# Batch 1's norm and transposes moved ahead, high parts multiplied first, and a gate buffer for each batch in the scan stage of a decoder layer

## What is computed

```python
x = x + _L0_attn_ref(_layernorm(x), W_in, conv_w, conv_b, W_g, b_g, forget_base, W_out)
# inside, H = 384:
gx = einsum('ntd,hd->nth', x, W_in);  gate, xb = gx[..., :H], gx[..., H:]
xb = depthwise_causal_conv(xb, conv_w, conv_b)            # 4 taps along t
fg = einsum('nth,gh->ntg', xb, W_g) + b_g;  forget, inp = fg[..., :H], fg[..., H:]
alpha = exp(-8 * softplus(forget_base) * sigmoid(forget))
beta = sqrt(1 - alpha ** 2 + 1e-6)
h = linear_scan(alpha, beta * sigmoid(inp) * xb)          # h[t] = alpha[t] h[t-1] + x[t]
return einsum('nth,dh->ntd', gelu(gate) * h, W_out)
# then: cross attention (AFT, local) with its MLP, and two layers of windowed attention with MLP
```

## Time and profile before

| what | us |
|---|---|
| median of three runs | 992.8 |
| lowest and highest run | 991.03, 993.05 |
| span of the profiled execution (its own whole time is not listed) | 990.8 |
| PE busy in the span | 924.9 |
| DVE, ACT, POOL busy | 675.9, 513.9, 422.6 |

### The profile page before, as it was taken

One profiled execution on the slowest core, in us unless ns is written; L12 is line 12 of the kernel. 1 busy time (PEld: TensorE's weight loads), 2 busy tenths in 40 slices (PEclk: granted clock), 3 DMA queues, 4 the chain that ended last, 5 costly groups with the idle time before them and its releaser, 6 DMA issues.

```text
span 990.8 us, 17519 instructions
## 1 busy us (share of the span) xinstructions
PE 924.9 (93%) x5688; PEld 774.2 (78%) x5688; DVE 675.9 (68%) x1706; ACT 513.9 (52%) x1221; POOL 422.6 (43%) x420
## 2 busy tenths in 40 slices
PE   5889996999999988999999899999999999889998
PEld 4668875787878866888888678887888888778887
DVE  6878797558687677677767555567766667735563
ACT  5467751313131426767666644454766666654443
POOL 5333354112221357767676400006776767631110
PEclk9889998999999999999999999999999999999999
DMA  7200123000000000000001030000000000000001
GB/s 261 70 1 16 48 65 112 1 1 0 0 0 1 1 23 1 2 23 0 22 0 33 12 105 15 4 25 2 2 24 0 22 0 12 27 15 17 31 25 46
DMA packets 15716, 26.34 MB, mean 27 GB/s; under 512 B 1642, under 2 KB 12256, under 8 KB 14896
## 3 DMA queue, kind: packets, MB, share of 16 engines
q1 hardware_dynamic: 15664, 25.69, 8.0%
HBM read 20.53 MB, written 2.10 MB: 23 GB/s over the span
## 4 chain that ended last, share of the span: by engine, by line
PE 72%; DVE 11%; ACT 6%; issue 3%; POOL 3%; SPq 3%; DMA 2%; ACTq 0%; DVEq 0%; POOLq 0%
PE bank L1593 33%; PE bank L1941 5%; PE bank L1895 5%; PE bank L1919 5%; PE bank L1801 5%; PE bank L1905 4%; ACT probs L1460 3%; PE bank L1764 2%; PE bank L1882 2%; PE bank L1747 1%; SPq L352 1%; DVE y L820 1%; PE bank L1929 1%; PE bank L2014 1%; PE bank L2011 1%
## 5 line engine op out<-in xcount | busy, mean ns | idle before, releaser
L1460 ACT ACTIVATE probs<-bank,row_min 128x256 f32<-128x256 f32 (+1 forms) x256 | 110.4, 458 | 120.1 <-DVE row_min L1048 120.1
L569 POOL TENSOR_TENSOR norms<-norms,minus_half 128x16 f32<-128x16 f32 x32 | 93.6, 2924 | 2.7
L1048 DVE CUSTOM_DVE_ANT_0 bank<-bank,mask 128x256 f32<-128x256 f32 (+1 forms) x256 | 90.7, 425 | 5.9 <-PE bank L1895 5.7
L1593 PE MATMUL bank<-wqkv_hi,x_hi 128*128 128x512 f32 x192 | 82.4, 429 | 1.8 <-DVE rot L1024 1.1
L1593 PE MATMUL bank<-wqkv_lo,x_hi 128*128 128x512 f32 x192 | 76.3, 397 | 0.0
L1593 PE MATMUL bank<-wqkv_hi,x_lo 128*128 128x512 f32 x192 | 75.7, 394 | 0.0
L1185 DVE SCALAR_TENSOR_TENSOR hidden<-bank,lcols,hidden 128x512 f32<-128x512 f32 (+1 forms) x48 | 36.0, 749 | 51.9 <-PE bank L1593 28.2
L551 POOL TENSOR_TENSOR q_tok<-rot 128x512 f32<-128x512 f32 x32 | 41.2, 1288 | 57.7 <-DVE rot L1024 57.7
L1905 PE MATMUL bank<-ident,probs 128*128 128x128 f32 x448 | 61.5, 279 | 3.9 <-ACT probs L1460 3.9
L1593 PE MATMUL bank<-t_hi,wm_hi 128*128 128x512 f32 x160 | 63.6, 397 | 0.0
L1593 PE MATMUL bank<-t_lo,wm_hi 128*128 128x512 f32 x160 | 63.5, 397 | 0.0
(11 more groups left out here) (253 smaller groups left out, 2639.5 us busy)
## 6 DMA issues: line engine op xcount, KB each, us to landing
w_stage<-in_wm_l_dram SPq DMA_DIRECT2D x8, 534.0 KB, 3.7
w_stage<-in_wqkv_dram SPq DMA_DIRECT2D x2, 1536.0 KB, 8.0
out_dram<-stream SPq DMA_DIRECT2D x8, 256.0 KB, 2.4
emb<-in_ctx_dram SPq DMA_DIRECT2D x1, 1536.0 KB, 6.8
inner<-in_w_gate_dram SPq DMA_DIRECT2D x1, 1152.0 KB, 10.3
stream<-in_x_dram SPq DMA_DIRECT2D x2, 512.0 KB, 5.7
stream<-in_x_dram SPq DMA_DIRECT2D x1, 1024.0 KB, 12.8
ew<-in_pos_bias_dram SPq DMA_DIRECT2D x1, 1024.0 KB, 11.5
```

The source lines that it names most:

```text
L569: pool.tensor_tensor(norms[:, 2, :], norms[:, 1, :], minus_half[:, :], ALU.pow).then_inc(c_rn, 1)
L1048: dve.tensor_tensor_reduce(logits, logits, mask[:, 2 * P - nk:2 * P], 1.0, FAR, ALU.add, ALU.min, row_min[:, w % 2, 2 * i + e:2 * i + e + ...
L1460: act.activation(probs[:, i, e, 0:nk], logits, ACT.Exp, bias=row_min[:, w % 2, h:h + 1], scale=-1.0, accum_out=row_sum[:, w % 2, h:h + 1]) ...
L1593: ins = pe.matmul(out, stationary, moving, start=(first and i == 0), stop=(last and i == len(terms) - 1))
```

## The change

It has five parts.

1. The gate has four buffers, one for each batch. The two new ones are slices of `w_stage`, which holds nothing in this stage (its first transfer waits for the last `output`). ACT's wait for `a_gh` is gone.
2. Batch 1's `norm_stats` and `rstd_of` stand earlier, and so does its `norm_apply`. POOL begins the split of the gate weight only when all of batch 1 is normed (`n_norm`, 2 * TT).
3. PE transposes batch 1 after the fourth input product of batch 0, no longer after the sixth. ACT rounds it into `t_hi` before the last gelu of batch 0, after waiting for all of batch 0's input products, which read `t_hi`.
4. The first input product of every batch (`first_input`) multiplies the four pairs with a high part of the tokens first, and the two with the low part last. It waits for each part by itself; before, all six waited for both low parts. Batch 0's transposes go token tile by token tile, each as soon as its tile is normed.
5. DVE takes `conv_taps(0, 2)` ahead of `conv_low(0, 0)`.

```diff
+        gate_acts = [gate_act[:, i, :, :] for i in range(2)]
+        gate_acts += [w_stage[:, i * KR * T:(i + 1) * KR * T].rearrange(...) for i in range(2)]
...
             rstd_of(0)
+            rstd_of(1)
+            pool.wait_ge(n_norm, 2 * TT)
             pool.wait_ge(wg_in, 16)
             for k in range(KR):
-                if k == 1:
-                    rstd_of(1)
                 raw_k = w_raw[:, WIN_COLS + k * 2 * RH:WIN_COLS + (k + 1) * 2 * RH]
...
                 if i == 1:
                     low_part(0, a_tp_out, a_tp_lo)
-
-            dve.wait_ge(x1_in, 16)
-            dve.wait_ge(a_tp, 2)
-            norm_stats(1, 1)
+                    dve.wait_ge(x1_in, 16)
+                    norm_stats(1, 1)
+
+            dve.wait_ge(a_tp, KD)
+            norm_apply(1, 1, False)
...
-            norm_apply(1, 1, False)
             conv_taps(0, 0)
             conv_taps(0, 1)
             low_part(1, a_tp_out, a_tp_lo)
+            conv_taps(0, 2)
             conv_low(0, 0)
-            conv_taps(0, 2)
             conv_low(0, 1)
...
-            def gelu_gate(b):
-                if b > 1:
-                    act.wait_ge(a_gh, 3 * b - 3)
-                for j in range(KR):
+            def gelu_gate(b, js=range(KR)):
+                for j in js:
                     act.wait_ge(a_in, 6 * b + KR + j + 1)
-                    act.activation(gate_act[:, b % 2, j, :], ...)
+                    act.activation(gate_acts[b][:, j, :], ...)
...
             taps(0)
-            gelu_gate(0)
+            gelu_gate(0, range(KR - 1))
+            act.wait_ge(a_in, 2 * KR)
             transposed_out(1)
+            gelu_gate(0, range(KR - 1, KR))
...
+            def first_input(b, m):
+                for k in range(KD):
+                    pe.wait_ge(a_tp_out, KD * b + k + 1)
+                    if b == 0:
+                        pe.wait_ge(win_hi, k + 1)
+                    pe.matmul(bank[2], w_in_hi[:, k, m], t_hi[:, k], start=(k == 0), stop=False)
+                for k in range(KD):
+                    if b == 0:
+                        pe.wait_ge(win_lo, k + 1)
+                    pe.matmul(bank[2], w_in_lo[:, k, m], t_hi[:, k], start=False, stop=False)
+                for k in range(KD):
+                    pe.wait_ge(a_tp_lo, KD * b + k + 1)
+                    ins = pe.matmul(bank[2], w_in_hi[:, k, m], t_lo[:, k], ..., stop=(k == KD - 1))
             def inputs(b):
-                pe.wait_ge(a_tp_lo, 2 * b + 2)
                 for j in range(2 * KR):
+                    if b == 0 and j == 4:
+                        transpose_in(1)
```

More of the change, by code:

```diff
@@ L145, in build @@
         gate_act = sb("gate_act", [P, 2, KR, T], stack=st1)
+        gate_acts = [gate_act[:, i, :, :] for i in range(2)]
+        gate_acts += [w_stage[:, i * KR * T:(i + 1) * KR * T].rearrange("p (j t) -> p j t", j=KR) for i in range(2)]
         th_in = sb("th_in", [P, KR, T], stack=st1)
@@ L426, in gate_products @@
                     pool.wait_ge(a_scan, 3 * b + j + 1)
-                    pool.tensor_tensor(scanned[:, j, :], scanned[:, j, :], gate_act[:, b % 2, j, :], ALU.mult)\
+                    pool.tensor_tensor(scanned[:, j, :], scanned[:, j, :], gate_acts[b][:, j, :], ALU.mult)\
                         .then_inc(a_gh, 1)
@@ L749, in recurrence @@
                     dve.wait_ge(a_scan, 3 * b + j + 1)
-                    dve.tensor_tensor(scanned[:, j, :], scanned[:, j, :], gate_act[:, b % 2, j, :], ALU.mult)\
+                    dve.tensor_tensor(scanned[:, j, :], scanned[:, j, :], gate_acts[b][:, j, :], ALU.mult)\
                         .then_inc(a_gh, 1)
@@ L1274, in taps @@
                         .then_inc(a_tap0, 1)
-            def gelu_gate(b):
-                if b > 1:
-                    act.wait_ge(a_gh, 3 * b - 3)
-                for j in range(KR):
+            def gelu_gate(b, js=range(KR)):
+                for j in js:
                     act.wait_ge(a_in, 6 * b + KR + j + 1)
-                    act.activation(gate_act[:, b % 2, j, :], bank[2 + (KR + j) % 4][:, :], ACT.Gelu).then_inc(a_gelu, 1)
+                    act.activation(gate_acts[b][:, j, :], bank[2 + (KR + j) % 4][:, :], ACT.Gelu).then_inc(a_gelu, 1)
             act.wait_ge(w1s_in, 16)
@@ L1597, in transpose_in @@
             def transpose_in(b):
-                pe.wait_ge(n_norm, 4 * b + 4)
-                for c in range(KD):
-                    for t in range(TT):
+                if b:
+                    pe.wait_ge(n_norm, 4 * b + 4)
+                    pe.wait_ge(a_tp_lo, KD * b)
+                    for c in range(KD):
+                        for t in range(TT):
+                            ins = pe.transpose(bank[c][:, t * P:(t + 1) * P], normed[:, t, c * P:(c + 1) * P],
+                                               ident[:, :])
+                        ins.then_inc(a_tp, 1)
+                    return
+                for t in range(TT):
+                    pe.wait_ge(n_norm, t + 1)
+                    for c in range(KD):
                         ins = pe.transpose(bank[c][:, t * P:(t + 1) * P], normed[:, t, c * P:(c + 1) * P],
                                            ident[:, :])
-                    ins.then_inc(a_tp, 1)
+                        if t == TT - 1:
+                            ins.then_inc(a_tp, 1)
+            def first_input(b, m):
[3 more added lines that the diff above has]
+                        pe.wait_ge(win_hi, k + 1)
+                    pe.matmul(bank[2][:, :], w_in_hi[:, k, m * P:(m + 1) * P], t_hi[:, k, :], start=(k == 0), stop=False)
+                for k in range(KD):
+                    if b == 0:
+                        pe.wait_ge(win_lo, k + 1)
+                    pe.matmul(bank[2][:, :], w_in_lo[:, k, m * P:(m + 1) * P], t_hi[:, k, :], start=False, stop=False)
+                for k in range(KD):
+                    pe.wait_ge(a_tp_lo, KD * b + k + 1)
+                    ins = pe.matmul(bank[2][:, :], w_in_hi[:, k, m * P:(m + 1) * P], t_lo[:, k, :], start=False,
+                                    stop=(k == KD - 1))
+                ins.then_inc(a_in, 1)
             def inputs(b):
-                pe.wait_ge(a_tp_lo, 2 * b + 2)
                 for j in range(2 * KR):
                     m = (j + KR) % (2 * KR)
+                    if b == 0 and j == 4:
+                        transpose_in(1)
                     if b == 1 and j < 2:
@@ L1618, in inputs @@
                         pe.wait_ge(a_tap0, 3 * b + j - 4 + 1)
-                    if b == 0 and j % KR == 0:
-                        pe.wait_ge(win_lo, KD * (j // KR + 1))
+                    if j == 0:
+                        first_input(b, m)
+                        continue
+                    if b == 0 and j == KR:
+                        pe.wait_ge(win_lo, 2 * KD)
                     product(bank[2 + j % 4][:, :], [
@@ L1667, in _ @@
             inputs(0)
-            transpose_in(1)
             inputs(1)
```

## The result

The changed kernel takes 983.66 us, the median of four runs (982.97 to 986.82), beside 991.91 us (989.44 to 993.05) for the kernel before, also four runs. The comparison gives a ratio of 0.9942, with a 95% interval of 0.9922 to 0.9961. That is 5.7 us faster, by the interval 3.9 to 7.7. The two medians by themselves lie further apart, 8.2 us. I had forecast 6.5 us and 986.3 us, with a range of 982.0 to 990.2. The profiled execution has a span of 981.2 us.

The account below looks back on a forecast made before the run. PE, busy for 93% of the span, was taken as the bound, with time to gain only in its idle and half-clock stretches. Gate buffers 5.4 + front 1.1 = 6.5 us, so 992.8 - 6.5 = 986.3 us; range 982.0 to 990.2.

Parts of the forecast that it names:

- The bound: Scan stage: PE works 93% of the span, so time can come only where it idles or runs at half clock.
- Part 1: Gate buffers: the 2.95 us gelu wait and 2.9 of half clock go, a 0.4 wait comes; gain 5.4 us.
- Part 2: Batch 1's norm comes 7.0 us earlier, but POOL's split then blocks DVE's taps; t_lo ends at 29.2, so nothing is gained.
- The rule of the page: Front taps: under an exclusive DVE/GpSimd port lock, t_lo of batch 1 is ready at 30.4, the forecast about 0.6 us later.
- POOL's split: Gate-weight split on POOL: delayed to about 25.5 from 22.85 us; PE needs it at 38, so nobody waits.
- Parts 3 and 4: Front, batch 1's input products: four matmuls run before the pause, the end comes at 38.1 instead of 39.2; gain 1.1 us.
- Part 5: Taps before conv_low: conv_lo ready at about 35.2, long before PE's 38.1; costed at nothing.
- The sum: Whole program: 5.4 + 1.1 = 6.5 us, from 992.8 to 986.3 us.
- DVE holds batch 1: Rival, chance 0.14: PE waits at batch 3's transposes, the gate buffers bring only 2.95; sum 4.0, 988.8 us.
- Nothing is left: Rival, chance 0.09: front loses 1.0 us, gate buffers keep 2.95 less 1.5 for DVE late at batch 3; 992.3 us.
- Slower: Rival, chance 0.05: POOL's split makes DVE 8.1 us late to batch 3's norm, PE waits 2.7 us; 995.5 us.
- The front opens: Rival, chance 0.08: taps blocked little, t_lo ready before PE asks, front brings up to 7.5; sum 12.9, 979.9 us.

Follow-up runs that it names:

- e6: The changed kernel without POOL's three subtractions for the gate weight's low part, which is set to zero and missing from the result: 978.42 us, ratio 0.9882.
- e8: The changed kernel with the gate-weight split taken off POOL: ACT rounds, DVE subtracts, and POOL makes batch 2's rstd earlier: 978.28 us, ratio 0.9880.
- e1: The kernel before with only the four gate buffers added and ACT's wait for a_gh removed: 986.14 us, ratio 0.9951.
- e3: The kernel before with twelve more matmuls, result unused, where PE waits for batch 2's gelu; the wait itself stays: 988.37 us, ratio 0.9984.
- e4: The changed kernel without POOL's wait for n_norm ahead of the gate-weight split: 984.92 us, ratio 0.9934.
- e7: The changed kernel with POOL's gate-weight split put off until DVE has made its first six taps: 980.65 us, ratio 0.9902.
- e2: The changed kernel with the two old gate buffers and ACT's wait for a_gh put back: 988.92 us, ratio 0.9977.
- e5: The changed kernel with each batch's first input product waiting for both t_lo before any of its matmuls: 986.19 us, ratio 0.9958.

## Why the prediction was right, step by step

- **The bound.** Right. Both places that I named are where the runs find the time: the front (up to 6 us more, e6 to e8) and the gelu wait (5.1 us, e1).
- **Part 1, 5.4 us forecast.** The traces show 5.1 from `gates(0)` to `output(0)`, in the changed kernel and in e1. The terms: the wait of 2.95 is gone. The half clock cost 2.6 (2.55 by e3), where I had 2.9. I took 27 x 0.234 from 9.19 and left out two things that full clock has too: the second matmul after a pause starts 0.34 us behind the first (67.48 to 67.82 in e3), 0.1 more than the 0.234 of the others, and the last of a row ends 0.39 us after its start, which adds 0.16. Together these are the 0.3. The new wait for `normed` is 0.47, where I had 0.4.
- **Part 2, nothing left of 7.0 us.** Right, with two misses that cancel, so that 29.2 is closer than its terms. `normed` ended at 16.79, not 16.0: the statistics began at 11.84, not 11.5, and POOL's `var_eps` and `rstd` took 0.41 and 1.21 us, not the 1.2 together that they took before (0.19 and 1.01). They stand beside `w_in_lo`, which I had put there myself and at no cost. The block of the taps cost less than I took. From the end of `normed` to the end of the taps it is 11.34 us (16.79 to 28.13), where I had 11.95. POOL's first rounding (0.84) met only the little `fb_tmp`, which lost 0.6 us. `t_lo` ended at 29.32 us, forecast 29.2. That 29.2 was right for the reason given is shown by e4 (the same 29.46 with the block on `normed`) and by e6 and e7 (the block taken away).
- **The rule of the page.** By the Trainium skill, "SBUF — State Buffer", a blocked instruction of DVE's, with two inputs in SBUF as the taps have, would start only after the whole of the other, and `t_lo` would have come at 30.4. The first tap ended 0.56 us after POOL, near (0.53), not 0.75, and `t_lo` came at 29.32. The trace agrees with the page on the block, and not on its last 0.2 us.
- **POOL's split.** Forecast to end at 25.5, it ended at 26.57. 0.8 us of that is its later start (16.88, not 16.1). Here a step failed: I said only that the block lengthens DVE. POOL is lengthened as well, 0.84 to 1.29 and 1.85 to 2.15 us, when it comes while a tap of DVE's is under way. Its six durations add up to 9.5 us instead of 8.1. My 25.5 had 1.3 us more than 16.1 + 8.1, for which I gave no term. This cost nothing, as said, since PE reads the split only at 38 us.
- **Parts 3 and 4, 1.1 us forecast.** `gates(0)` came at 38.31 us, forecast 38.1, and 39.18 before: 0.87 us earlier. Four matmuls at 23.31 to 24.67, the rest from 28.78, half clock until 32.9: all within 0.2 us of the steps. Some of this is luck. That the same half-clock stretch would follow was an assumption, and e3, e1 and e2 show that it need not: with the old front `gates(0)` stood at 38.57 to 39.76, with the new one at 38.31 and 38.75. The means of the three and of the two lie 0.6 us apart, so one pair of traces does not show the 0.87. What doesn't hang on the clock is the part that e5 takes out, 1.5 us for high parts first.
- **Part 5, nothing.** `conv_lo` of batch 0 was ready at 35.51 us (forecast 35.2), before PE's 38.31. It was not tried alone.
- **The sum.** 5.1 + 0.87 = 6.0 us at `output(0)`, and 6.0 at `output(1)`. The ratio says 5.7 (3.9 to 7.7), and I had 6.5. Of the 0.5 between the traces and that, 0.3 are the terms of part 1 that I left out, and 0.2 are at `gates(0)`.
- **The rivals.** "DVE holds batch 1" fell with the wait of 0.47 us at batch 3. "Nothing is left" and "Slower" fell with it: DVE was at most half a microsecond late there. "The front opens" was wrong for this change, but its price was about right. Where the block is taken off the taps (e6, e8), the kernel is 11.7 and 11.9 us faster, and I had priced it at 12.9.
- **The absolute time.** 983.66 us is 2.6 below 986.3, more than the miss of the sum. What failed here is the level that I subtracted from. 992.8 was the median of three runs. The kernel before had 990.74 in 24 runs beside e1 to e4 and 989.89 in 17 beside e5 to e8. I also took the 2.0 us from the profiled span to the median for time that lies around the span. It isn't: in every run that lists both, 1.7 to 1.9 us lie around it, so the profiled execution before took about 992.6 us (estimated from 990.8), and was one of the long ones. The clock goes with this. In the 24 runs, those with a mean granted clock of 0.981 took 992.4 to 993.8 us, and those with 0.988 to 0.990 took 987.6 to 988.6. Before was profiled at 0.981, the changed kernel at 0.990. So the span fell by 9.6 us between the profiled executions, not 6.0, and the other 3.6 us are not the change's as far as anything here shows. 1.5 of them lie from `output(1)` on, where before had a stretch of half clock at 135.3 us that the changed kernel does not have (1.00 in the table above), and 1.3 at the next one, which lasted 10.2 us before (from 166.0) and 6.8 in the changed kernel (from 159.3). This is the first one's row in the table by stretch of before:

```profile
135.30:138.70 3.40, 3.40 (x8) 2.71 (x9) 3.40 (x3) 0.52 (x2) 2.66 (x1) 0.50 0.50 207
```

PE's work there was not touched. None of the eight experiments' profiles has this stretch either, those with the old gate buffers (e2, e3) among them. But before was profiled only once, so whether it usually falls there stays open.

## What to carry to other kernels

When DVE and GpSimd both work from SBUF, moving one of DVE's instructions out of the way can hand the block to the next one, as it did here. Ask what stands beside the split after the move, and put it beside reads of a bank or work that nobody waits for (e7), or on another engine (e8). A short wait of TensorE can cost nearly twice its length (2.95 us and 2.6 of half clock here): look at the granted clock behind each pause, and where the data can't come sooner, start the products that don't need it. Before you read a microsecond out of one pair of traces, look at how far the same unedited stretch moves between executions: here it was 1.2 us.

## What the runs showed of the hardware

- The block between GpSimd and VectorE works both ways. POOL's rounding of 768 columns took 0.84 us alone (e7, 21.68 us) and 1.27 to 1.29 us beside taps, and its subtraction 1.85 beside reads of a bank and 2.12 to 2.16 beside taps. In e4, beside `normed` (256 columns), they took 0.83 to 0.89 and 1.80 to 1.85, that is, hardly more. The tap is the longer instruction (0.75 us against 0.41) and also reads two tensors from SBUF, not one. Which of the two lengthens POOL's was not tried.
- Work that reads one of its operands from a bank was not blocked. In e7 POOL's first `w_gate_lo` (22.61 us, 1.85 long) ran while DVE took `t_lo` from a bank (22.55 to 23.84 us), and neither was lengthened: `t_lo` kept its 1.29 us.
- The half clock behind a pause does not come in one length. Behind the pause of the front it lasted 6.8 us in before, the changed kernel, e1, e2 and e5 (pauses of 4.80, 4.11, 4.67, 4.96 and 5.34 us), and 3.4 us in e3 (3.92) and e4 (2.08, with pauses of 1.88 and 0.78 in the eight us before it). Behind the same gelu wait of 2.95 us it was 6.8 in before and 3.4 in e2. Single pauses of 1.2 to 1.5 us between 29 and 61 us brought none in any of these profiles. For a forecast that counts on one length, the two at the gelu wait differ by 1.1 us.
